# Macaron block on one core: attention's norm in one piece with four first projections, its last products turned about, and another order at the edges of the feed-forward layers

## The chip, the cores and the metric

One core of a Trainium2 chip. The metric is the device time of one execution in microseconds, median of three runs. One core has five engines with queues of their own: TensorE (PE, with its weight loads, PEld), VectorE (DVE), ScalarE (ACT), GpSimd (POOL) and SyncE (SP, here only DMA issues).

## The reference

A "macaron" block on x of 2 batches × 512 tokens × 512:

```python
x = x + 0.5 * ffn(layernorm(x))
x = x + attention(layernorm(x))      # 32 heads of 128, 8 KV heads, causal, no positions
x = x + 0.5 * ffn(layernorm(x))      # the same weights again
...
def ffn(x2):                          # 1024 tokens
    g_s, u_s = split(x2 @ shared_w_gate_up.T)              # 512 wide each
    shared_out = silu(g_s) * u_s @ shared_w_down.T
    w = top2(softmax(x2 @ gate_w.T)); w = w / sum(w)        # 16 experts
    moe_out = sum_e w_e * (silu(g_e) * u_e @ w_down_e.T)    # 128 wide each
    return moe_out + shared_out
```

Everything is float32.

## The kernel before

Each float32 product is made of three fp32r products of split operands, `PARTS = ((0,0),(0,1),(1,0))`: a "high" part, which ScalarE makes by a copy (`..._hi`), and a "low" part, the difference, which DVE or POOL subtracts (`..._lo`). So each product has, in front of it, a copy and a subtraction on two other engines. PSUM has eight banks, each named in the code.

x lies in SBUF as 8 tiles of 128 tokens (tiles 0 to 3 are batch 0, 4 to 7 batch 1). Each of the five engines runs a program written out by hand in one block (`block.tensor`, `.vector`, `.scalar`, `.gpsimd`, `.sync`); the order in each is the order of issue, and semaphores with counted values tie them together. Nothing is scheduled by a planner.

**A feed-forward layer** (n = 0 before attention, n = 1 behind it). The norm goes in two halves (`normalise`, L832 to 854; `turn_norm` on TensorE, L1188; `turned_norm` on ScalarE L571 and DVE L864). The shared part has 8 slots s: slice s//2 of the inner width and batch s%2. For each: `gate_up` (gate half, then up half, 12 matmuls each, L1252), silu (`gate`, ACT L608), `multiply` (DVE L969), `high` (ACT L614), `low` (DVE L974), `down` (12 matmuls, 3 for each tile, L1271), `add_down` (DVE, four adds, L962). A slice's weights are cut by `cut_gu` and `cut_dn` (ACT L592, L599) and `low_gu`, `low_dn` (DVE L941, L948; POOL L465, L471), from `raw_w[0]` or `raw_w[1]`, into one pair of buffers `wgu`, `wdn` (slice 3's down weights into `wdn_late`). Slots 0 to 4 come before the routed tiles, 5 to 7 behind them.

The router's logits are matmuls (`router`, L1199), copied by ScalarE (L578), folded and turned by 16 small matmuls (L1210), which lie between the router and `gate_up(1)`; DVE finds the top two (L881 to L895), `rank` (L1284, L1288, issued in the second half of `gate_up(1)`) counts, DVE makes row numbers (L905 to L916). POOL scatters the normalised tokens to `x_rows` in DRAM by 16 indirect DMAs (L509), TensorE goes on with shared slots 2 to 4, and then come 31 tiles of 128 sorted rows (`routed`): SP loads a tile into `xn` (L331), TensorE turns it (L1299), ScalarE copies (`turned`, L634) and DVE subtracts (L997), the expert's weights are cut as a front part (ACT L638, DVE L1003) and a back part (ACT L644, POOL `back` L481), gate and up (L1338), silu, product, `turn_hidden` (L1314), y (L1349), `y_out` (DVE L1021), store (SP L336). After the last tile POOL gathers the rows back by 16 indirect DMAs (L520), two for each tile of tokens, and DVE adds them with their weights (`combine`, L1044, two tiles of tokens to a call, m = 0 and 1 each). In the first layer POOL stops after the 12th gather until 8 combine adds are done, makes four of the six low parts of attention's first weights (`first_cuts`, L545; the key's, the value's and four queries' weights), then issues the last four gathers and the two low parts left.

The order on TensorE behind the tiles:

```python
gate_up(n, BEFORE + 1)                 # slot 5
pe.wait_ge(moe[n].y_out, TILES)
down(n, BEFORE)                        # slot 4
gate_up(n, SLOTS - 2)                  # slot 6
gate_up(n, SLOTS - 1, (0,))            # slot 7, gate
down(n, SLOTS - 2)
gate_up(n, SLOTS - 1, (1,))            # slot 7, up
down(n, BEFORE + 1)
if n == 0:
    turn_norm(1, 0)
down(n, SLOTS - 1)
```

**Attention** has 64 units u (8 KV heads × 2 batches × 4 query heads) in a software pipeline of slots (`att_slots`: the first and last written out, a loop between). In slot u TensorE does: scores S(u) (L1394, L1398), turns of unit u-1's probabilities (L1376), the projection of a later query (L1363), the last turns of u-1, the dense product of an earlier unit (L1432, 12 matmuls into one token tile of x), PV of u-1 (L1444, L1448), and in some slots the projection of a key or value. Masks and maxima are DVE's (L1071), exponentials ScalarE's (L732), the division POOL's (L538), the high and low parts of probabilities ACT L706 and DVE L1051, of queries and outputs ACT L711, L744 and DVE L1055, the dense adds DVE L1091. Ahead of slot 0: key, value, `project(wqs[0])` into bank 4 (after `add_down(7)`), the value's turn. After slot 1's PV: the norm's second half, `turn_norm(1, 1)`, in two pairs of tiles, which wait for each other's low parts, and behind it key 1.

SP issues the weights of layer 1 once the last in-loop product is done (o_mm ≥ 64), on both sides of the change.

## Time and profile before

| | us |
|---|---|
| median of 3 runs (1162.78 to 1164.62) | 1164.51 |
| the profiled execution, its own time | 1161.62 |
| its span, first to last instruction | 1159.9 |
| TensorE busy | 1110.0 |
| DVE busy | 670.8 |
| ScalarE busy | 571.6 |
| POOL busy | 465.4 |

The mean granted clock of TensorE is 0.988 of full. A row of a timeline has start, duration, engine, line, operation, what is written from what is read, and in brackets the idle time of the engine before it and what ended it. "issue" there is time in which the engine waited for nothing that the profile shows, "remote" a release that comes from none of the recorded instructions. A start is counted from the span's first instruction. Matmul ends are modelled.

### The profile page before, as it was taken

What the parts mean: (1) busy time and instruction counts of PE and PEld (TensorE: products, weight loads), DVE (VectorE), ACT (ScalarE), POOL (GpSimd) and SP (SyncE); (2) the same over time, 40 slices, a digit from 0 to 9 for tenths busy, and PEclk for the clock granted to TensorE, in tenths of its full rate; (3) what the DMA queues carried; (4) which work ended last, traced back from release to release, by engine and by line L of the source; (5) the groups of instructions that cost most, each with busy time, mean ns of one, the idle gap of its engine ahead of it and who ended that gap; (6) DMA issues with size and microseconds to landing.
All of it is one profiled execution on the core that took longest, in us unless ns stands there. A gap on an engine that the chain in (4) does not pass through costs nothing.

```text
span 1159.9 us, 19606 instructions
## 1 busy us (share of the span) xinstructions
PE 1110.0 (96%) x6008; PEld 930.1 (80%) x6008; DVE 670.8 (58%) x1810; ACT 571.6 (49%) x1514; POOL 465.4 (40%) x484
## 2 busy tenths in 40 slices
PE   8889998799999999999999999999999998899996
PEld 6667876588888888888888888888888876678875
DVE  7568867744545444545454445454454547668866
ACT  4257752555546445545444454544553533257750
POOL 1546647125315315324423432522532320546644
PEclk9989999999999999999999999999999999999998
DMA  9985565001101101000110010010000006935556
GB/s 357 414 325 190 186 225 185 16 1 37 56 1 37 55 0 36 22 32 0 36 54 0 36 54 0 36 54 0 36 0 1 1 1 269 372 112 176 189 157 197
DMA packets 38617, 114.80 MB, mean 99 GB/s; under 512 B 4384, under 2 KB 4384, under 8 KB 36512
## 3 DMA queue, kind: packets, MB, share of 16 engines
q1 hardware_dynamic: 33440, 97.30, 23.1%
q0 software_dynamic: 5120, 16.78, 4.2%
q8 instruction: 30, 0.49, 0.2%
q14 instruction: 27, 0.22, 0.1%
HBM read 79.20 MB, written 34.87 MB: 98 GB/s over the span
## 4 chain that ended last, share of the span: by engine, by line
PE 89%; DVE 4%; issue 3%; ACT 2%; DMA 1%; DVEq 0%; SPq 0%; ACTq 0%
PE bank L1363 23%; PE bank L1432 15%; PE bank L1448 9%; PE bank L1398 9%; PE bank L1338 7%; PE bank L1252 6%; PE bank L1376 6%; PE bank L1349 4%; PE bank L1271 3%; PE bank L1299 2%; PE bank L1444 1%; PE bank L1394 1%; DMA xn<-x_rows 1%; PE bank L1231 1%; PE bank L1188 1%
## 5 line engine op out<-in xcount | busy, mean ns | idle before, releaser
L538 POOL TENSOR_TENSOR scores<-scores,pinv 128x512 f32<-128x512 f32 (+3 forms) x256 | 176.7, 723 | 360.6 <-DVE pinv L1081 360.6
L481 POOL TENSOR_TENSOR tback_lo<-experts,tback_hi 128x768 fp32r<-128x768 f32 x62 | 114.3, 1845 | 82.4 <-ACT tback_hi L644 82.4
L744 ACT ACTIVATE oT_hi<-bank 128x512 fp32r<-128x512 f32 x64 | 38.3, 598 | 208.7 <-PE bank L1444 208.7
L732 ACT ACTIVATE scores<-scores,nmax 128x512 f32<-128x512 f32 (+3 forms) x256 | 140.3, 558 | 0.6 <-DVE nmax L1071 0.5
L706 ACT ACTIVATE pT_hi<-bank 128x512 fp32r<-128x512 f32 (+2 forms) x192 | 86.8, 487 | 108.0 <-PE bank L1376 108.0
L1051 DVE TENSOR_TENSOR pT_lo<-bank,pT_hi 128x512 fp32r<-128x512 f32 (+2 forms) x192 | 100.9, 553 | 48.3 <-ACT pT_hi L706 48.3
L1071 DVE CUSTOM_DVE_ANT_0 scores<-bank,causal 128x512 f32<-128x512 f32 (+3 forms) x256 | 112.2, 486 | 1.5 <-issue 0.5
L1363 PE MATMUL bank<-xnT_hi,wqs_hi 128*128 128x512 f32 x256 | 106.4, 416 | 0.9 <-DVE x L962 0.9
L1432 PE MATMUL bank<-wds_hi,oT_hi 128*128 128x512 f32 x256 | 105.9, 414 | 1.4 <-DVE oT_lo L1055 1.4
L1055 DVE TENSOR_TENSOR oT_lo<-bank,oT_hi 128x512 fp32r<-128x512 f32 x64 | 44.3, 691 | 108.6 <-ACT oT_hi L744 108.6
L1363 PE MATMUL bank<-xnT_lo,wqs_hi 128*128 128x512 f32 x256 | 100.8, 394 | 0.0
L1363 PE MATMUL bank<-xnT_hi,wqs_lo 128*128 128x512 f32 x256 | 100.8, 394 | 0.0
L1432 PE MATMUL bank<-wds_hi,oT_lo 128*128 128x512 f32 x256 | 100.6, 393 | 0.0
L1432 PE MATMUL bank<-wds_lo,oT_hi 128*128 128x512 f32 x256 | 99.5, 389 | 0.0
L1376 PE MATMUL bank<-ident,scores 128*128 128x128 f32 x640 | 90.8, 272 | 2.4 <-DVE pT_lo L1051 2.4
L1376 PEld LDWEIGHTS bank<-ident,scores 128*128 128x128 f32 x640 | 75.4, 141 | 11.0 <-DVE pT_lo L1051 2.8
L1091 DVE TENSOR_TENSOR x<-bank,x 128x512 f32<-128x512 f32 x64 | 44.1, 691 | 64.8 <-PE bank L1432 64.8
L1398 PE MATMUL bank<-kT_hi,qT_hi 128*128 128x512 f32 (+2 forms) x192 | 73.1, 381 | 2.2 <-DVE qT_lo L1055 2.2
L545 POOL TENSOR_TENSOR wqs_lo<-raw_q,wqs_hi 128x512 fp32r<-128x512 f32 x32 | 41.3, 1295 | 76.1 <-ACT wqs_hi L680 75.1
L1448 PE MATMUL bank<-pT_hi,vv_hi 128*128 128x512 f32 (+2 forms) x192 | 65.5, 341 | 1.6 <-DVE pT_lo L1051 1.6
L1398 PE MATMUL bank<-kT_hi,qT_lo 128*128 128x512 f32 (+2 forms) x192 | 65.1, 339 | 0.0
L1448 PE MATMUL bank<-pT_hi,vv_lo 128*128 128x512 f32 (+2 forms) x192 | 65.0, 339 | 0.0
(206 smaller groups left out, 2885.2 us busy)
## 6 DMA issues: line engine op xcount, KB each, us to landing
experts<-in_ffn_w SPq DMA_DIRECT2D x32, 768.0 KB
xn<-x_rows SPq DMA_DIRECT2D x62, 256.0 KB, 2.7
y_rows<-xn SPq DMA_DIRECT2D x62, 256.0 KB, 2.1
raw_q<-in_wq SPq DMA_DIRECT2D x8, 1024.0 KB
raw_d<-in_wd SPq DMA_DIRECT2D x8, 1024.0 KB
x_rows<-experts SPq DMA_DIRECT2D x1, 7936.0 KB, 29.7
raw_w<-in_ffn_w SPq DMA_DIRECT2D x8, 768.0 KB, 5.6
raw_kv<-in_wkv SPq DMA_DIRECT2D x8, 512.0 KB, 3.3
```

Of the source, the lines that this page charges most:

```text
L481: nc.gpsimd.tensor_tensor(tback[par][1][:], experts[:, bass.ds(at + FRONT, GU - FRONT)], tback[par][0][:].bitcast(F32), ALU.subtract).then ...
L538: nc.gpsimd.tensor_tensor(s, s, pinv[k % 2][:, i:i + 1].to_broadcast([P, P * (i + 1)]), ALU.mult).then_inc(att.normed, 1)
L706: nc.scalar.activation(pT[0][:, lo_col:hi_col], bank[b][:, 0:hi_col - lo_col], ACT.Copy).then_inc(att.t_hi, 1)
L732: nc.scalar.activation(s, s, ACT.Exp, bias=nmax[par][:, i:i + 1], scale=-1.0, accum_out=psumr[par][:, i:i + 1]).then_inc(att.exp, 1)
L1051: nc.vector.tensor_tensor(pT[1][:, lo_col:hi_col], bank[b][:, 0:hi_col - lo_col], pT[0][:, lo_col:hi_col].bitcast(F32), ALU.subtract).then ...
L1071: nc.vector.tensor_tensor_reduce(sp_[par][:, TRI[i]:TRI[i + 1]], bank[bk][:, c:c + w], causal[:, 512 - w:512], -SCORE_SCALE, 3.0e38, ALU.a ...
L1338: last = nc.tensor.matmul(bank[par][:, 0:2 * INTER], xT[par][a][:, c, :], piece[b][:, start:start + FRONT], start=(i == 0), stop=(i == 3 * ...
L1363: last = nc.tensor.matmul(into[:], w[a][:, c, :], xnT[z][:, c, b * SEQ:(b + 1) * SEQ], start=(m == 0), stop=(m == 3 * HC - 1))
L1376: last = nc.tensor.transpose(bank[b][:, at + (i - j) * P:at + (i - j + 1) * P], sp_[par][:, TRI[i] + j * P:TRI[i] + (j + 1) * P], ident[:])
L1398: last = nc.tensor.matmul(bank[bk][:, c:c + P * (i + 1)], qT[a][:, i * P:(i + 1) * P], kT[b][z][:, 0:P * (i + 1)], start=(m == 0), stop=(m ...
L1432: last = nc.tensor.matmul(o_bank(u)[:], oT[ob][h][a][:, tile * P:(tile + 1) * P], wds[h][z][:], start=(m == 0), stop=(m == 3 * G - 1))
L1448: last = nc.tensor.matmul(bank[1][:, j * P:SEQ], vv[bu][a][:, j, :], pT[z][:, COL[j]:COL[j] + SEQ - j * P], start=(j == 0 and m == 0), sto ...
```

## The change

It alters the order of work, buffers and semaphore counts, and the engine that makes six low parts; matmuls are as many as before.

- Router: the logits' banks are 1 and 4 (before 1 and 3); the 16 fold matmuls are issued after the first three matmuls of `gate_up(1)`, and `rank` one chunk later.
- Start of the tiles: the back part of tile 2 is cut ahead of the steps by ScalarE and POOL, `cut_dn(2)` moves to step 1, `add_down(3)` is split, two tiles of it in step 0. SP issues the loads of tiles 6 and 7 sooner, between experts' loads, and the raw weights of slice 3 before the tile loop; slice 3's gate and up weights have buffers of their own (`wgu_late`), cut at the last tile.
- End of the tiles and behind: the orders below. The six low parts of attention's first weights are DVE's (`first_lows`), and POOL's 16 gathers have no pause in them.
- Attention's start: key, value, queries 0 and 1 are projected into banks 0, 3, 1 and 2, the value is turned, `turn_norm(1, 1)` goes in one piece in banks 4 to 7, then come the slots; key 1 is projected in slot 0, query 2 in slot 1.
- Attention's end: from unit 63 on the dense product stands before the last turns, the wait for the last output's low part (`pv_lo`) comes only before its head, and the tail is cut by the norm of the next layer: slots 65 and 66, `turn_norm(2, 0)`, slots 67 and 68. The first gate and up of layer 1 wait for 61 and 63 adds (before 61 and 64).
- End of layer 1: `add_down(7)` in two pairs of tiles, about the combines; the stores of output tiles 2 and 3 wait for the combine adds.

```diff
-                    if j <= TILES - 2:
+                    if 0 < j <= TILES - 2:
...
@@ SP
-                for e in left[3:]:
+                for e in left[3:5]:
                     load_expert(e)
-                for k in range(4):
+                load_tile(n, 1, 2)
+                for e in left[5:]:
+                    load_expert(e)
+                store_tile(n, 0, 0)
+                load_tile(n, 1, 3)
+                for k in range(1, 4):
                     store_tile(n, 0, k)
-                    if k < 2:
-                        load_tile(n, 1, k + 2)
+                load_shared(n, 3)
                 with sp.Fori(2, TILES // 4) as it:
@@ POOL
                 back(0, at[1], 1)
+                back(1, at[2], 2)
                 low_dn(n, BEFORE // 2)
...
-                    if n == 0 and t == HALF + 1:
-
-                        pool.wait_ge(moe[n].added, 2 * HALF)
-                        first_cuts(low_part, 0, G)
...
-            pool.wait_ge(ffn[0].act_lo, SLOTS)
-            first_cuts(low_part, G)
+            pool.wait_ge(ffn[0].dn_lo, NSH)
@@ ACT, routed
                 front(at[1])
+                act.wait_ge(ffn[n].act_lo, BEFORE)
+                act.wait_ge(ffn[n].d_mm, HALF * (BEFORE - 1))
+                back(1, at[2], there[2] if n == 0 else 2 * LOADED_HALF)
                 turned(0, 1)
-
-                cut_dn(n, BEFORE // 2)
                 tile_steps(step)
@@ ACT, feed_forward
                 high(n, BEFORE)
-                shared(n, BEFORE + 1, SLOTS - 2)
+                gate(n, BEFORE + 1)
+                gate(n, SLOTS - 2)
+                cut_dn(n, NSH - 1)
                 if n == 0:
                     act.wait_ge(loaded.kv, 16)
                     first_cuts(high_part, 0, 2)
-                shared(n, SLOTS - 2, SLOTS - 1)
-                if n == 0:
                     act.wait_ge(loaded.q, 16)
                     first_cuts(high_part, 2)
+                high(n, SLOTS - 2)
+                high(n, BEFORE + 1)
                 gate(n, SLOTS - 1)
+                high(n, SLOTS - 1)
                 if n == 0:
                     roots(1, 0)
-                high(n, SLOTS - 1)
@@ DVE, feed_forward
                 multiply(n, BEFORE)
                 routed(n)
                 low(n, BEFORE)
+                if n == 0:
+                    first_lows(0, 2)
+                multiply(n, SLOTS - 2)
+                low_dn(n, NSH - 1)
+                if n == 0:
+                    first_lows(2, 4)
+                low(n, SLOTS - 2)
+                if n == 0:
+                    first_lows(4, 2 + G)
                 multiply(n, BEFORE + 1)
-                low_gu(n, NSH - 1)
                 low(n, BEFORE + 1)
-                low_dn(n, NSH - 1)
                 combine(n, 0)
-                multiply(n, SLOTS - 2)
-                low(n, SLOTS - 2)
+                add_down(n, SLOTS - 2)
+                multiply(n, SLOTS - 1)
                 combine(n, 2)
-                add_down(n, SLOTS - 2)
 
             feed_forward(0)
-            then = statistics(1, 0)
-            multiply(0, SLOTS - 1)
-            scaled(1, 0, then)
             low(0, SLOTS - 1)
+            normalise(1, 0)
             turned_norm(1, 0)
...
@@ PE, gate_up
+                if s == 1:
+
+                    pe.wait_ge(route[n].out, 1)
...
-                        if half == 1 and s == 1 and c == 1:
+                        if half == 0 and s == 1 and c == 1:
+                            fold_logits(n)
+                        if half == 1 and s == 1 and c == 2:
                             rank(n)
@@ PE, last tile step
                     if isinstance(j, int) and j == TILES:
+                        gate_up(n, BEFORE + 1, (0,), range(0, HC // 2))
                         turn_hidden(j, par)
+                        gate_up(n, BEFORE + 1, (0,), range(HC // 2, HC))
@@ PE, attention slot (dense is the old block as a function)
-                        if r == 1:
-                            pe.wait_ge(att.pv_lo, u - 1)
...
+                            if r == 1 and h == G - 1:
+                                pe.wait_ge(att.pv_lo, u - 1)
...
+                    if isinstance(u, int) and u == 0:
+                        pe.wait_ge(norm[1].lo, TT)
+                        project(wks, 1, PROJ_AHEAD)
+                    elif exists(u, 0, UNITS - 2):
...
+                    if isinstance(u, int) and u >= UNITS - 1:
+                        dense(g, u, k)
                     if exists(u, 1, UNITS):
                         pe.wait_ge(att.t_lo, 3 * (u - 1) + 1)
                         turn(1 - par, 2, 6, 0)
                         turn(1 - par, 3, 6, 256).then_inc(att.t_mm, 1)
...
-                    if isinstance(u, int) and u == 1:
-
-                        pe.wait_ge(att.proj_out, before + QPOS[1] + 1)
-                        turn_norm(1, 1)
-                        pe.wait_ge(norm[1].lo, TT)
@@ PE, attention
-                pe.wait_ge(ffn[0].added, HALF * (BEFORE + 2))
-                project(wqs[0], 0, 0, bank[4])
-                turn_value(2)
+                project(wqs[0], 0, 0, bank[1])
+                pe.wait_ge(att.w_lo, 4)
+                project(wqs[1], 0, 0, bank[2])
+                pe.wait_ge(att.v_first, 1)
+                turn_value(1)
+                turn_norm(1, 1)
                 att_slots(pe, slot)
-                att_tail(slot)
+                att_tail(slot, 1, 2)
+                turn_norm(2, 0)
+                att_tail(slot, 3, 4)
@@ PE, feed_forward
-                gate_up(n, BEFORE + 1)
+                gate_up(n, SLOTS - 2)
 
                 pe.wait_ge(moe[n].y_out, TILES)
                 down(n, BEFORE)
-                gate_up(n, SLOTS - 2)
-                gate_up(n, SLOTS - 1, (0,))
+                gate_up(n, BEFORE + 1, (1,))
                 down(n, SLOTS - 2)
-                gate_up(n, SLOTS - 1, (1,))
+                gate_up(n, SLOTS - 1)
                 down(n, BEFORE + 1)
+                down(n, SLOTS - 1, range(0, HALF // 2))
                 if n == 0:
                     turn_norm(1, 0)
-                down(n, SLOTS - 1)
+                down(n, SLOTS - 1, range(HALF // 2, HALF))
```

DVE's part of attention's start, of its end (`normalise(2, 0)`, slots 65 and 66, `turned_norm(2, 0)`, slots 67 and 68) and of the last layer (`low(7)`, `combine(4)`, half of `add_down(7)`, `combine(6)`, the other half) follows TensorE's order.

## Rows read from the trace of the kernel before

**Rows 1.** The page, busy time of each engine and the chain by engine
```profile
PE 1110.0 (96%) x6008; PEld 930.1 (80%) x6008; DVE 670.8 (58%) x1810; ACT 571.6 (49%) x1514; POOL 465.4 (40%) x484
...
PE 89%; DVE 4%; issue 3%; ACT 2%; DMA 1%; DVEq 0%; SPq 0%; ACTq 0%
```

**Rows 2.** Windows: stretch, us; each engine's busy us (count); granted clock; DMA share; GB/s
```profile
200.20:257.20 57.00, 49.57 (x258) 40.84 (x257) 35.93 (x109) 27.98 (x76) 12.04 (x17) 0.97 0.07 28
...
257.20:930.00 672.80, 672.80 (x3608) 580.27 (x3607) 334.08 (x1080) 334.93 (x997) 252.98 (x306) 1.00 0.07 25
```

**Rows 3.** Timeline of POOL, first scatter: start, us, instruction, idle before it
```profile
54.63 0.97 POOL L509 DMA_INDIRECT x_rows<-xn,rows  x1 [0.30 <-issue]
```

**Rows 4.** Timeline of ScalarE, first scatter
```profile
58.22 0.60 ACT L608 ACTIVATE sg<-bank 128x512 f32<-128x512 f32 x1 [7.23 <-remote]
```

**Rows 5.** Chain of waits in order of time, its long pieces: start, us, what
```profile
37.09 5.59 PE bank L1252 x24
...
172.64 8.39 PE bank L1252 x36
...
231.85 4.38 PE bank L1363 x12
```

**Rows 6.** Timeline of ScalarE, first gather
```profile
186.50 0.60 ACT L608 ACTIVATE sg<-bank 128x512 f32<-128x512 f32 x1 [2.66 <-remote]
```

**Rows 7.** Timeline of POOL, first gather
```profile
171.84 1.29 POOL L520 DMA_INDIRECT yg<-y_rows,rows  x1 [0.31 <-issue]
...
183.60 1.03 POOL L520 DMA_INDIRECT yg<-y_rows,rows  x1 [0.30 <-issue]
```

**Rows 8.** Timeline of ScalarE, second gather
```profile
1137.76 0.60 ACT L608 ACTIVATE sg<-bank 128x512 f32<-128x512 f32 x1 [0.87 <-issue]
```

**Rows 9.** Timeline of DVE, second gather
```profile
1147.41 0.69 DVE L969 TENSOR_TENSOR sg<-sg,bank 128x512 f32<-128x512 f32 x1 [3.77 <-remote]
```

**Rows 10.** Timeline of POOL, second gather, its first and last transfer
```profile
1125.70 0.99 POOL L520 DMA_INDIRECT yg<-y_rows,rows  x1 [9.69 <-DMA y_rows<-xn]
...
1146.13 0.95 POOL L520 DMA_INDIRECT yg<-y_rows,rows  x1 [0.30 <-issue]
```

**Rows 11.** Timeline of TensorE, first routed tiles
```profile
75.78 0.36 PE L1338 MATMUL bank<-tfront_hi,xT_hi 128*128 128x256 f32 x1 [1.94 <-DVE tfront_lo L1003]
...
87.89 0.66 PE L1299 MATMUL bank<-ident,xn 128*128 128x128 f32 x4 [0.95 <-DMA xn<-x_rows]
```

**Rows 12.** Timeline of TensorE, norm ahead of attention
```profile
194.19 3.43 PE L1188 MATMUL bank<-ident,xn 128*128 128x128 f32 x16 [3.03 <-DVE xn L854]
```

**Rows 13.** Timeline of DVE, ahead of that norm
```profile
186.55 2.48 DVE L962 SCALAR_TENSOR_TENSOR x<-bank,x 128x512 f32<-128x512 f32 x4 [1.42 <-PE bank L1271]
...
189.07 2.47 DVE L832 BATCH_NORM_STATS2 stats<-x 128x6 f32<-128x512 f32 x4
```

**Rows 14.** Timeline of TensorE, attention's start
```profile
211.22 0.50 PE L1398 MATMUL bank<-kT_hi,qT_hi 128*128 128x512 f32 x1 [0.90 <-DVE qT_lo L1055]
...
217.44 0.50 PE L1398 MATMUL bank<-kT_hi,qT_hi 128*128 128x512 f32 x1 [1.34 <-DVE qT_lo L1055]
...
226.26 0.39 PE L1448 MATMUL bank<-pT_hi,vv_hi 128*128 128x256 f32 x1 [1.65 <-DVE pT_lo L1051]
...
229.22 1.22 PE L1188 MATMUL bank<-ident,xn 128*128 128x128 f32 x8 [1.23 <-DVE xnT_lo L864]
...
231.85 0.79 PE L1363 MATMUL bank<-xnT_hi,wks_hi 128*128 128x512 f32 x1 [1.41 <-DVE xnT_lo L864]
```

**Rows 15.** Timeline of TensorE, attention's end
```profile
951.93 0.55 PE L1376 MATMUL bank<-ident,scores 128*128 128x128 f32 x3 [1.25 <-DVE pT_lo L1051]
...
958.46 0.50 PE L1432 MATMUL bank<-wds_hi,oT_hi 128*128 128x512 f32 x1 [1.41 <-DVE oT_lo L1055]
...
972.78 0.48 PE L1231 MATMUL bank<-xnT_hi,wgu_hi 128*128 128x512 f32 x1 [1.40 <-issue]
```

**Rows 16.** Timeline of POOL, attention's end
```profile
946.85 2.76 POOL L538 TENSOR_TENSOR scores<-scores,pinv 128x512 f32<-128x512 f32 x4 [7.49 <-DVE pinv L1081]
```

More of the change, by code:

```diff
@@ L146, in build @@
                 yg = sb("yg", [P, TT, 2, HID], F32, sub)
-            oT = [[pair(f"oT0_{r}", [P, SEQ], st) for r in range(G)], [None] * G]
+            oT = [[None] * G, [pair(f"oT1_{r}", [P, SEQ], st) for r in range(G)]]
             pT = pair("pT", [P, TRI[ST]], st)
@@ L160, in build @@
             kT[1] = pair("kT1", [P, SEQ], st)
-            oT[1][0] = pair("oT1_0", [P, SEQ], st)
-            oT[1][1:] = [pair(f"oT1_{r}", [P, SEQ], st) for r in range(1, G)]
+            oT[0][G - 1] = pair(f"oT0_{G - 1}", [P, SEQ], st)
+            oT[0][:G - 1] = [pair(f"oT0_{r}", [P, SEQ], st) for r in range(G - 1)]
             vT = sb("vT", [P, SEQ], F32, st)
@@ L261, in att_slots, with att_tail @@
                 slot(KV - 1, k)
-        def att_tail(slot):
-            for k in range(8 + 1, 8 + 5):
+        def att_tail(slot, first, last):
+            for k in range(8 + first, 8 + last + 1):
                 slot(KV - 1, k)
         def o_bank(u):
-            return bank[(0, 1, 3, 2)[u - UNITS - 1] if isinstance(u, int) and u > UNITS else 2]
+            return bank[(0, 1, 2, 3)[u - UNITS - 1] if isinstance(u, int) and u > UNITS else 2]
         UNITS = KV * BATCH * G
@@ L603, in gate @@
                 act.wait_ge(f.g_mm, s + 1)
-                wait(act, f.act_lo, s - 1)
+                if s >= 2:
+                    act.wait_ge(f.act_lo, DOWN_AT[s - 2] + 1)
                 if s == 1:
@@ L1015, in step @@
                                                 ALU.mult).then_inc(m.mul, 1)
+                    if j == 0:
+                        add_down(n, BEFORE - 1, range(HALF // 2, HALF))
+                    if j == TILES:
+                        low_gu(n, NSH - 1)
                     if exists(j, 1, TILES):
@@ L1028, in routed @@
                 turned(0, 1)
-                add_down(n, BEFORE - 1)
+                add_down(n, BEFORE - 1, range(HALF // 2))
                 dve.wait_ge(route[n].scattered, 2 * TT * 16)
@@ L1184, in turn_norm @@
                     pe.wait_ge(norm[n].mul, t + 1)
-                    wait(pe, norm[n].lo, t - 1 if n == 1 and h == 1 else t - 3)
+                    if n != 1:
+                        wait(pe, norm[n].lo, t - 3)
                     for c in range(HC):
@@ L1378, in turn, with dense @@
                     return last
+                def dense(g, u, k):
+                    if exists(u, 5, UNITS + 4):
+                        r = k % 4
+                        ob = (0, 1, 1, 1, 1, 0, 0, 0)[k % 8]
+                        tile = (r - 1) % 4
+                        wait(pe, att.added, UNITS - HALF if isinstance(u, int) and u > UNITS else u - 5)
+                        m = 0
+                        for h in range(G):
+                            if k == 5:
+                                pe.wait_ge(att.w_lo, 6 + 10 * g + (3 if exists(u, 0, UNITS - 9) else 1) + h)
+                            if r == 1 and h == G - 1:
+                                pe.wait_ge(att.pv_lo, u - 1)
+                            for a, z in PARTS:
+                                last = nc.tensor.matmul(o_bank(u)[:], oT[ob][h][a][:, tile * P:(tile + 1) * P],
+                                                        wds[h][z][:], start=(m == 0), stop=(m == 3 * G - 1))
+                                m += 1
+                        last.then_inc(att.o_mm, 1)
                 def slot(g, k):
@@ L1391, in slot @@
                             wait(pe, att.masked, 4 * (u - 1) + (1, 3, 4)[n])
+                            if isinstance(u, int) and u == 0:
+                                wait(pe, norm[1].lo, (0, HALF + 1, HALF + 2)[n])
                             for i, c in tiles:
```

214 lines of the change are left out of this document (122 added, 92 removed).

## The prediction

> **What bounds the kernel now.** I read the page first. TensorE is busy for 1110.0 of 1159.9 us, and the chain that ended last is 89% TensorE [rows 1]; no other engine is above 58%. The change alters no matmul, so it can act only through TensorE's idle time, 50 us in all, and through its clock. The table of windows says where that is: none in attention's loop, where TensorE is busy for 672.80 of 672.80 us, and 7.4 us at attention's start [rows 2]; the rest is at attention's very end and in the two feed-forward layers. The timelines then give each wait a place and a releaser.
>
> One thing needs care before any sum. POOL issues the 16 indirect transfers of the first scatter, each 0.97 us with 0.30 between, the last at 54.63 [rows 3]. In the later part of such a run TensorE's signals seem to reach the others late. ScalarE's silu of shared slot 3 waits 7.23 us and starts at 58.22, just after the run, released by something that the trace calls remote [rows 4]. In the first gather, which began at about 169.3, a stretch of 36 matmuls ends at 181.03 (172.64 and 8.39) [rows 5]; the silu behind it starts only at 186.50, after a remote wait [rows 6], when POOL's pause had begun at 184.63 (183.60 and 1.03) [rows 7]. In the second gather, which has no pause, the silu at the same place starts at once, 12.1 us into the run (1137.76 against 1125.70), but DVE's last multiplication waits 3.77 us on something remote and starts at 1147.41, as the run ends (1146.13 and 0.95) [rows 8 to 10]. I read: late in a run TensorE's signals are held until the run ends or pauses; it began before 11.7 us in the first gather, after 12.1 in the second.
>
> **The change part by part.** One 512-column matmul costs 0.233 us (5.59 for 24 [rows 5]).
>
> *Router.* The 16 fold matmuls come three matmuls later, 0.7 us, and what covers the copy they wait for was idle time anyway. So row numbers, scatter and all that hangs on the scatter's end [rows 3, 4] come about 0.65 later in each layer: a loss of 1.3. Bounds: 0 (the restart does not follow) and -1.4.
>
> *Start of the routed tiles.* The weights of tile 2 are cut before the steps, and the adds of shared slot 3 are split in two. The 1.94 us wait for DVE's front part [rows 11] goes, but tile 2 waits for the same chain (copy of back(1), turned, POOL's back), and I leave it about half: +1.05 per layer. The tile load moved before the last experts takes away the 0.95 us wait for data at 87.89 [rows 11] in the first layer. Together +3.05. Bounds: 0, if tile 2 inherits all, and 2 × 1.94 + 0.95 = 4.8.
>
> *End of the first layer.* Before: gate-up 5, down 4, gate-up 6, gate 7, down 6, up 7, down 5, norm, down 7. After: gate 5 around the last tile's turn, gate-up 6, down 4, up 5, down 6, gate-up 7, down 5, half of down 7, norm, the other half. What ends last in both is DVE's work up to the first normalised row, for which TensorE stands 3.03 us and starts at 194.19 [rows 12]. The six subtractions of attention's first weights move from POOL to DVE (0.69 each, as its operations of this size [rows 9]), 4.1 us more, ahead of the adds. DVE's list from low 4 on is now fourteen operations of 0.69 (9.7), two combines of four such (2.75 each), four adds (2.48), four statistics (2.47) [rows 13] and 2.5 more to the first row (194.1 less the statistics' end at 191.54): 22.6 us. With its waits for gathers and ScalarE I get the first row at 194.8 against 194.1; but half of down 7 is then done before the norm, 1.4 us that stood behind it. If signals come in time, attention so starts some 0.4 earlier: +0.4. But the gather now has no pause. It starts 1.9 later, since gate 5 (2.8) stands before the last tile's product and not behind it, at 171.2, and its 16 transfers end at about 192 (15 × 1.27 + 0.95, one or two of them lengthened). The last multiplication stands on a signal of TensorE that leaves about 14.5 us into the run, and behind it in DVE's queue stand combine 2, low 7 and the norm: 0.7 + 2.75 + 0.7 + 5.0 = 9.1 us to the first row, so at 201, 6 later than in time. That gives 0.4 - 6 = -5.6. The lower bound, with add_down 6 held as well, is 3 us worse, -8.6; the upper is +0.4. I take -5.6, since the first gather already held a signal at 11.7 us [rows 5, 6].
>
> POOL's gathers and DVE meet here in another way: the transfer at 171.84 took 1.29 us [rows 7], while DVE subtracted two SBUF tensors; the last of the second gather took 0.95 [rows 10]. The Trainium skill (Trainium Architecture — The Big Picture, What this means for kernel authors) says that the port pair shared by DVE and GpSimd is an exclusive lock and not a split of bandwidth, and so speaks against the move of the six subtractions. The trace agrees for this one transfer. By that rule the six would lengthen the run by 6 × 0.34, some 2 us, and the sum would be as much smaller, which lies inside the bounds above.
>
> *Attention's start.* Four first projections (key, value, two queries) fill the stretch in which DVE ends the second half of x; then comes the norm of the other four tiles in one piece, and key 1 sits in slot 0. Gone are the waits of 0.90, 1.34, 1.65, 1.23 and 1.41 us, and the slow passage of key 1's 12 matmuls after them, 4.38 against 2.8 at the full clock: 1.6 [rows 5, 14]. That is 8.1. New: DVE's queue behind the first norm is eight combines (5.5), four adds, statistics and scaling (2.5, 2.5, 2.5), which ends some 1.9 us behind the four projections (48 matmuls, 11.2) and the value's turn; and S(1) waits for the low parts of the second query and of key 1, about 1.8. 8.1 - 3.7 = +4.4. Bounds: +1 (the norm's wait brings the half clock to what follows it, and each new wait is about a microsecond longer) and +6.2 (no wait at S(1)).
>
> *Attention's end.* Products before turns cover the 1.25 wait; the wait for the last head's low part, 1.41, comes behind 9 of 12 matmuls; the norm in the middle of the tail fills the 1.40 before the first gate [rows 15]: 4.06 at most. The slot before gains nothing: POOL's four divisions end at 949.61 (946.85 and 2.76) [rows 16], and the turn behind them can't be earlier. I take +3.3, bounds +1.4 and +4.1. The experts of the second layer are asked for at the same product as before and hide under its router.
>
> *End of the second layer.* The last multiplication's signal leaves earlier in the run (about 14.5 us instead of 17.8). In time, the end comes 1.8 earlier; held to the end of a run that starts 1.9 later and with adds split about the combines, 3.7 later. I take -0.4, between, since this gather held nothing at 12.
>
> **Sum.** -1.3 + 3.05 - 5.6 + 4.4 + 3.3 - 0.4 = +3.45 us. The profiled execution took 1161.6 us beside its span of 1159.9; the change's would take 1158.2. The runs' median is 1164.5, 2.9 above; less 3.45 that is 1161.1.
>
> The Trainium skill (TensorE: Matmul & The Clock Gate, Part 1: The HAM clock gate) puts it that the default state is throttled and activity releases the throttle. The 4.38 after idle fits [rows 5, 14]. By that rule any wait left at attention's start costs more than itself, which would put that part nearer its lower bound.
>
> **The rivals.**
> - *Signals come in time* in the unpaused gathers. For it: the second gather held nothing at 12.1 us. Against: the first did at 11.7. The sum is -1.3 + 3.05 + 0.4 + 4.4 + 3.3 + 1.8 = 11.65: 1152.9 us.
> - *Slower: the run without a pause holds DVE's queue to its end* in both layers, one mechanism at its two places: -8.6 and -3.7 instead of -5.6 and -0.4. The sum is -2.85: 1167.4 us. It decides once the two together cost over 9.5, the sum of the other parts. For it: the 7.23 us in the scatter, which is such a run [rows 4]. Against: the second gather [rows 8].
> - *Attention's start doesn't do what it says*: each removed wait comes back as the wait for the norm and at S(1), at half clock, +1 instead of +4.4. Total 0.05: 1164.5 us.
>
> **How the numbers follow.** Chances: my forecast 0.42, signals in time 0.28, slower by the hold 0.18, start unchanged 0.12. About 0.2% (2.3 us) is what a measurement of this kernel can tell from no change: 1162.2 to 1166.8. The forecast's own range, 1157 to 1165, has about a third above 1162.2, so faster is 0.29 + 0.28 = 0.57; same is 0.13 of the forecast, 0.08 of the unchanged start and 0.02 of the slower case, 0.23; slower is the rest, 0.20. The range goes from 1152, past the case in time, to 1167.5, past the slower one.
>
> **What the changed profile would show.** In the first gather 16 transfers without a pause from about 171, DVE's last multiplication at 191 to 195 with a remote wait, and the first projection at 205 to 207; if that is at 200, the rival in time holds. From the first projection to the third unit's scores 4.4 us less. The last slots and the first gate of the second layer 3.3 closer. The 1.94 wait gone, a smaller one at tile 2. The prediction is wrong if the signals are not tied to POOL's run at all, or if a split product or the moved loads of shared weights bring a wait into the tiles, where I put none.

## The result: 0.5% slower, and where the profile puts it

The changed kernel takes 1171.1 us (median of 20 runs) against 1165.4 us (20 runs): ratio 1.0047, interval [1.0032, 1.0063]. One run of each kernel was far slower than the rest (1836.98 and 1246.07 us) and is left out of the ratio. The forecast was 1161.1 and a range up to 1167.5; the sign was wrong and the time lies outside the range.

The page of the changed kernel, the same two rows as [rows 1]:

```profile
PE 1112.9 (95%) x6008; PEld 932.1 (80%) x6008; DVE 674.5 (58%) x1815; ACT 569.6 (49%) x1513; POOL 458.0 (39%) x478
...
PE 81%; DVE 5%; another core or an unknown queue 4%; issue 3%; ACT 3%; DMA 2%; POOL 0%; SPq 0%; DVEq 0%; ACTq 0%
```

TensorE works nearly as long as before, but the chain has a new part, 4% "another core or an unknown queue": time in which an engine waited and none of the recorded instructions released it. The windows of the changed kernel, cut at the first tile's turn, the last tile's turn, the first projection, the second layer's first gate, and again the two turns (columns as in [rows 2]):

```profile
0.00:71.70 71.70, 58.25 (x279) 45.91 (x280) 43.49 (x123) 24.41 (x38) 21.25 (x34) 0.93 0.93 359
71.70:160.95 89.25, 86.02 (x560) 69.06 (x558) 71.54 (x120) 63.31 (x146) 55.14 (x31) 0.98 0.64 222
160.95:211.64 50.69, 40.25 (x175) 31.44 (x173) 31.52 (x60) 15.40 (x29) 18.49 (x19) 0.87 0.51 187
211.64:974.78 763.14, 758.31 (x4066) 651.95 (x4064) 393.79 (x1254) 377.33 (x1112) 272.89 (x331) 1.00 0.07 24
974.78:1032.09 57.31, 48.67 (x220) 37.01 (x219) 34.87 (x101) 17.75 (x27) 18.51 (x18) 0.94 0.82 325
1032.09:1117.85 85.76, 84.50 (x559) 68.16 (x558) 72.54 (x120) 63.16 (x146) 54.52 (x30) 1.00 0.53 176
1117.85:1168.30 50.45, 36.89 (x158) 28.56 (x156) 26.78 (x43) 8.29 (x17) 17.20 (x17) 0.88 0.46 146
```

Beside them the lengths of the same stages before:

| stage | before | after | difference | forecast |
|---|---|---|---|---|
| layer 1, to the first tile | 69.5 | 71.7 | +2.2 | +0.65 |
| its tiles | 87.2 | 89.3 | +2.0 | -2.0 |
| its end, to the first projection | 43.4 | 50.7 | +7.3 | +5.6 |
| attention, to the next layer's first gate | 772.6 | 763.1 | -9.4 | -7.7 |
| layer 2, to the first tile | 55.0 | 57.3 | +2.3 | +0.65 |
| its tiles | 85.6 | 85.8 | +0.1 | -1.05 |
| its end | 46.5 | 50.5 | +4.0 | +0.4 |
| span | 1159.9 | 1168.3 | +8.4 | -3.45 |

Attention gives more than forecast; the two feed-forward layers lose it, and more. (The profiled execution before, 1161.6 us, lay 3.8 us below the median of its 20 runs, so the two traces differ by more than the medians do. Stages of single traces vary too: the first stage, with the same code as before, took 71.1 and 71.6 us in the traces of att_only and before_nopause below. A difference of 2 us in one stage is not told from that.) The longest waits stand at POOL's four runs of 16 transfers. ScalarE's timeline:

```profile
54.86 0.60 ACT L627 ACTIVATE sg<-bank 128x512 f32<-128x512 f32 x1 [7.69 <-remote]
59.93 1.06 ACT L610 ACTIVATE wgu_hi<-raw_w 128x1024 fp32r<-128x1024 f32 x1 [4.47 <-remote]
...
196.99 0.60 ACT L627 ACTIVATE sg<-bank 128x512 f32<-128x512 f32 x1 [13.42 <-remote]
...
1153.47 0.60 ACT L627 ACTIVATE sg<-bank 128x512 f32<-128x512 f32 x1 [13.64 <-remote]
```

TensorE's timeline, what it stands for behind them (the second row is a wait among the tiles, for tile 8's rows):

```profile
62.30 0.79 PE L1315 MATMUL bank<-xnT_hi,wgu_hi 128*128 128x512 f32 x1 [8.00 <-DVE wgu_lo L977]
...
96.77 0.66 PE L1362 MATMUL bank<-ident,xn 128*128 128x128 f32 x4 [2.62 <-DMA xn<-x_rows]
...
201.71 0.77 PE L1334 MATMUL bank<-wdn_late_hi,ab_hi 128*128 128x512 f32 x1 [7.22 <-DVE ab_lo L1013]
206.31 3.67 PE L1244 MATMUL bank<-ident,xn 128*128 128x128 f32 x16 [1.70 <-DVE xn L889]
...
1023.70 0.80 PE L1315 MATMUL bank<-xnT_hi,wgu_hi 128*128 128x512 f32 x1 [7.86 <-DVE wgu_lo L977]
...
1158.18 0.77 PE L1334 MATMUL bank<-wdn_late_hi,ab_hi 128*128 128x512 f32 x1 [8.70 <-DVE ab_lo L1013]
```

And on POOL the last transfer of the first scatter and of the first gather:

```profile
56.62 0.97 POOL L528 DMA_INDIRECT x_rows<-xn,rows  x1 [0.30 <-issue]
...
193.68 0.94 POOL L539 DMA_INDIRECT yg<-y_rows,rows  x1 [0.30 <-issue]
```

The order in the first gather is: the transfers end at 194.62, and 2.4 us later, at 196.99, the silu of slot 7 begins, whose matmuls were over at about 187. Behind the silu come on DVE the multiplication (197.62), which also needs the up half, over at about 190, then combine 2, low 7 and the norm, until TensorE turns it at 206.31; in [rows 12] that was 194.19. In the second gather the transfers end at 1150.88 and the silu begins at 1153.47, 2.6 us later. Before, it began at 1137.76 there [rows 8].

Not every late signal waits for the run's end. In the first scatter the silu of slot 3 starts at 54.86, 6.1 us after its matmuls (over at 48.74) but 2.7 us before the run ends (57.59); only the next signal, that of the up half, is held past the end, and with it the cut of weights at 59.93, for which TensorE stands until 62.30. The trace of before had such releases inside a run too: its DVE and ScalarE both end a remote wait at 50.35, with the run ending at 55.60. So "held until the run ends or pauses", as the prediction read it, is too simple: signals become late, by 5 us and more, some pass while the run goes on, and the last ones come behind it.

### The profile page after: what moved, and what is told of

It reads as the page before. It is cut to its first block, busy times and chain, and to the rows that moved or that the text cites. A ratio compares the mean times of both kernels' runs of the same rounds, so it can differ in the third digit from the quotient of the medians.

```text
span 1168.3 us, 19604 instructions
## 1 busy us (share of the span) xinstructions
PE 1112.9 (95%) x6008; PEld 932.1 (80%) x6008; DVE 674.5 (58%) x1815; ACT 569.6 (49%) x1513; POOL 458.0 (39%) x478
## 4 chain that ended last, share of the span: by engine, by line
PE 81%; DVE 5%; another core or an unknown queue 4%; issue 3%; ACT 3%; DMA 2%; POOL 0%; SPq 0%; DVEq 0%; ACTq 0%
PE bank L1428 22%; PE bank L1460 14%; PE bank L1529 9%; PE bank L1489 8%; PE bank L1403 7%; PE bank L1441 6%; PE bank L1414 4%; PE bank L1315 3%; PE bank L1362 2%; PE bank L1525 1%; PE bank L1485 1%; DVE x L1087 1%; PE bank L1288 1%; DMA xn<-x_rows 1%
## 5 line engine op out<-in xcount | busy, mean ns | idle before, releaser
L560 POOL TENSOR_TENSOR wqs_lo<-raw_q,wqs_hi 128x512 fp32r<-128x512 f32 x28 | 36.3, 1295 | 75.2 <-ACT wqs_hi L703 75.2
L1414 PE MATMUL bank<-experts,hT 128*128 x124 | 64.5, 601 | 0.6 <-ACT hT L675 0.3
```

What stands on the lines that cost most here:

```text
L1414: last = nc.tensor.matmul(bank[6 + 1 - par][:], hT[:], experts[:, bass.ds(at[k] + GU, HID)], start=True, stop=True)
```

## The experiments

All ratios are to the kernel before, timed beside each on the same chip, where its median was 1165.2 to 1168.2 us. The changed kernel was not timed again there. A difference from it, or between two of the kernels below, is therefore taken between their two ratios (0.001 is 1.2 us) and carries the error of both, some 3 to 5 us.

**1 and 2. The change in two halves.** One kernel has only attention's edges (the norm in one piece with four first projections, the products turned about, the norm in the tail), the other all the rest. In short:

```diff
 att_only: before, with these
+                project(wqs[0], 0, 0, bank[1]); project(wqs[1], 0, 0, bank[2])
+                turn_value(1); turn_norm(1, 1)
...
+                att_tail(slot, 1, 2); turn_norm(2, 0); att_tail(slot, 3, 4)
 ffn_only: before, with every other hunk of the diff
```

> The kernel before with attention's two edges alone changed (four first projections, the norm in one piece, the products turned about, the norm within the tail); the feed-forward layers keep their order. Theory (the loss is all in the feed-forward layers, since POOL's runs of transfers hold TensorE's signals): attention's edges gave 9.4 us between the first projection and the next layer's first gate (763.1 against 772.6), so 9 us faster than before, ratio 0.992. Rival (attention's new start only looks quick because it begins after a longer stand, with more of DVE's work already behind it): 3 to 5 us faster.

> The rest of the change alone: router, start of the tiles, order behind them, the first weights' low parts on DVE, no pause in the gather; attention as before. Theory: the two layers lost 11.4 and 6.4 us, so 15 to 18 us slower than before, ratio 1.014. Rival (the loss comes from the two halves together): under 8 us slower.

att_only: 1156.9 us, ratio 0.9934 [0.9912, 0.9955], 7.7 us faster. ffn_only: 1181.5 us, ratio 1.0142 [1.0107, 1.0177], 16.5 us slower. The gain at attention's edges is real and stands alone (its trace has 761.8 us for that stage, as the changed kernel has 763.1); the loss is all in the feed-forward layers' part. In sum, 8.8, the halves lose 3 us more than the whole, which is within the error of the three ratios.

**3. A pause in the gathers.**

```diff
                         ).then_inc(gathered[t], 16)
+                    if t == HALF + 1:
+                        pool.wait_ge(moe[n].added, 2 * HALF)
```

> The changed kernel with POOL stopping after the 12th of its 16 gathers, in both layers, until eight combine adds are done, as the first layer did before; nothing else. Theory (a run holds the signals until it pauses): the silu of slot 7 starts about 2 us after the 12th transfer, near 191.5 instead of 197 in the first layer, and as much earlier in the second; 5 to 8 us faster than the changed kernel. Rival (the signals are late for another reason, such as TensorE's instruction fetch or traffic): the silu stays at 197 and the kernel gets 0 to 4 us slower by the late gathers.

1165.9 us, ratio 0.9996 [0.9976, 1.0017], 6 us faster than the changed kernel. Its timelines, POOL and then ScalarE:

```profile
191.40 0.95 POOL L539 DMA_INDIRECT yg<-y_rows,rows  x1 [0.30 <-issue]
198.56 1.15 POOL L539 DMA_INDIRECT yg<-y_rows,rows  x1 [6.21 <-DVE x L1089]
```

```profile
194.32 0.60 ACT L629 ACTIVATE sg<-bank 128x512 f32<-128x512 f32 x1 [7.42 <-remote]
```

The 12th transfer ends at 192.35, the silu starts 2.0 us later, with four transfers still to come; in the second layer it is 1145.90 and 1147.96. So it is the run on POOL that holds the signal, and a pause lets it through.

**4. A pause in the scatters**, until the first eight have landed.

```diff
                             in_=xn[:, t, :], in_offset=None).then_inc(route[n].scattered, 16)
+                    if t == HALF - 1:
+                        pool.wait_ge(route[n].scattered, 2 * HALF * 16)
```

> The changed kernel with POOL stopping after the 8th of the 16 scatters, in both layers, until those eight have landed; nothing else. Theory (a run holds the signals): the silu of slot 3 and what follows are released within about 2 us of the matmuls' end, TensorE's stand of 8 us before slot 4 shrinks to 1 or 2, though the scatter ends 2 to 3 us later and the first tile may wait for it; 4 to 10 us faster in all. Rival: the stands stay at 8 us and the scatter's end is later, 4 to 6 us slower.

1171.6 us, ratio 1.0051 [1.0030, 1.0072]: no gain. But the mechanism shows. ScalarE has no remote wait in the scatter any more, and slot 4 no stand. What takes its place is the first tile's data:

```profile
56.79 0.97 POOL L528 DMA_INDIRECT x_rows<-xn,rows  x1 [9.69 <-DMA x_rows<-xn,rows]
```

```profile
71.22 1.09 PE L1364 MATMUL bank<-ident,xn 128*128 128x128 f32 x4 [10.05 <-DMA xn<-x_rows]
```

Eight transfers took 9.7 us more to land, the scatter ended at 66.7 and no longer at 57.6, and TensorE waits 10.05 us for the tile (in the second layer the eight took 8.0). The theory held, the remedy was too long; my expectation of 2 to 3 us for the landing was wrong.

**5 and 6. Short pauses**, made by waiting for the very signals that would be held. On the changed kernel in all four runs, on att_only in the scatters and the second gather (there after the 10th and the 14th).

```diff
                             in_=xn[:, t, :], in_offset=None).then_inc(route[n].scattered, 16)
+                    if t == HALF:
+                        pool.wait_ge(ffn[n].g_mm, 4)
+                    if t == HALF + 1:
+                        pool.wait_ge(ffn[n].u_mm, 4)
...
                         ).then_inc(gathered[t], 16)
+                    if t == HALF:
+                        pool.wait_ge(ffn[n].g_mm, 8)
+                    if t == HALF + 1:
+                        pool.wait_ge(ffn[n].u_mm, 8)
```

> The changed kernel; in each of the two scatters POOL waits after the 10th transfer for TensorE's signal of slot 3's gate and after the 12th for that of its up half, and in each of the two gathers at the same places for slot 7's. These signals are due at that moment anyway, so that the waits are short if a pause lets them through. Theory: the stands of 8.0 and 7.9 us before slot 4 fall to about 2 to 3, those of 7.2 and 8.7 before down 7 to about 2 to 4; 12 to 18 us faster than the changed kernel, near 1155. Rival (only a pause until the transfers have landed helps, or the pauses cost as much as they save): within 4 us of it.

> The kernel with attention's two edges alone changed, and the same waits of POOL in the two scatters and, in the second layer, after the 10th gather and the 14th. Theory: the stands of 7.1 and 5.0 us before slot 4 and of 3.8 before down 7 shrink to a third; 8 to 12 us faster than without the waits (1156.9), near 1147. Rival: within 2 us of it.

after_selfwait: 1148.1 us, ratio 0.9849 [0.9812, 0.9886]: 23 us faster than the changed kernel, more than expected. att_selfwait: 1146.2 us, ratio 0.9836 [0.9797, 0.9875], 11 us faster than att_only. The pause is 2 us long, and ends with the signal. POOL and ScalarE in after_selfwait, first scatter:

```profile
53.16 0.96 POOL L528 DMA_INDIRECT x_rows<-xn,rows  x1 [1.94 <-remote]
```

```profile
52.92 0.60 ACT L635 ACTIVATE sg<-bank 128x512 f32<-128x512 f32 x1 [4.32 <-remote]
```

With the hold eased, the two orders of the feed-forward layers are 2 us apart (ratios 0.9849 and 0.9836), which is not told from nothing; without, 13 us (1.0047 and 0.9934). So some 12 us of the change's loss are the hold, which the new order runs into.

**7. The short pauses in the gathers alone.**

> The changed kernel with POOL's two short waits for TensorE's signals in the two gathers only; the scatters run through as in the change. Theory (both kinds of run hold signals, the gathers' hold is what the change made worse): 10 to 13 us faster than the changed kernel, near 1159, and the rest of the 23 us of the run with waits in all four belongs to the scatters, which the kernel before had too. Rival (the gain is the scatters'): 3 to 5 us faster.

1160.0 us, ratio 0.9935 [0.9910, 0.9959]: 13 us faster than the changed kernel. The other 10 us are the scatters', and the kernel before has such a hold in them too [rows 4].

**8. The pause taken from the kernel before.**

```diff
-                    if n == 0 and t == HALF + 1:
-                        pool.wait_ge(moe[n].added, 2 * HALF)
-                        first_cuts(low_part, 0, G)
...
+            first_cuts(low_part, 0, G)
             pool.wait_ge(ffn[0].act_lo, SLOTS)
```

> The kernel before with one edit: POOL's pause after the 12th gather of the first layer is gone, and the four low parts made in it follow the last gather. Theory (the run then holds slot 7's silu to about 191.5 instead of 186.5, but in this order DVE takes the multiplication only at 192, behind the statistics): within 2 us of before. Rival (the lost pause alone makes the loss of the first layer): 5 to 8 us slower.

1169.5 us, ratio 1.0019 [0.9999, 1.0040], 2 us slower, at the edge of what can be told. The held signal is not the expected one: the silu of slot 7 comes in time, at 186.32. The hold now stands elsewhere, at the adds of slot 6:

```profile
191.65 0.69 DVE L959 SCALAR_TENSOR_TENSOR x<-bank,x 128x512 f32<-128x512 f32 x1 [2.84 <-remote]
```

The old order has its multiplication of slot 7 behind the statistics, where a held signal has time; the changed one has it ahead of combine 2 and the norm. How the loss divides between the pause and the order stays open. By the medians the missing pause costs 2 us. By this trace the end of the first layer is 49.1 us long, 5.6 more than before (the changed kernel's is 50.7), and the attention stage behind it gives 2.4 of that back (770.2 against 772.6). Set back into the changed kernel (experiment 3), the pause brings that end to 45.8.

**9. POOL's run interrupted by POOL itself.** After every fourth transfer four small memsets, each waiting for the one before, 1.06 us in all, and no wait for another engine.

```diff
+                    if t % 2:
+                        for i in range(4):
+                            wait(pool, breathed, taken[0])
+                            nc.gpsimd.memset(breath[:], float(i)).then_inc(breathed, 1)
+                            taken[0] += 1
```

> The changed kernel; after every fourth transfer of each run POOL makes four small memsets, each waiting for the one before (some 1 us in all), and waits for no other engine. Theory A (any interruption of POOL's run lets TensorE's signals through): the silu of slot 7 starts by 191 instead of 197, the stands before slot 4 and down 7 fall to under 4 us, 8 us or more faster than the changed kernel. Theory B (the signals pass only in a pause of about 2 us, or when fewer transfers are under way): the stands stay and the longer runs make it 2 to 6 us slower.

1156.9 us, ratio 0.9899 [0.9873, 0.9925], 17 us faster than the changed kernel, though each run is 3 us longer. Its trace has no remote wait at all. The silu of slot 7:

```profile
186.57 0.60 ACT L640 ACTIVATE sg<-bank 128x512 f32<-128x512 f32 x1 [3.50 <-PE bank L1328]
```

So nothing in TensorE's work or its queue made the signals late, and no other engine need be waited for: in this run 1.2 us without a transfer's issue every 5 us were enough. What in the issue of transfers holds the signals, this doesn't show.

**10. Where slice 3's weights are loaded.** Behind the tile loop (after_sh3); and, with the short pauses, behind the row load of the last tile (combo1).

```diff
-                load_shared(n, 3)
                 with sp.Fori(2, TILES // 4) as it:
...
                     if k < TILES % 4:
                         load_tile(n, last, k)
+                    if k == TILES % 4 - 1:
+                        load_shared(n, 3)
```

> The changed kernel with the load of slice 3's weights behind the tile loop on SyncE's queue, and no longer ahead of the load of tile 8. Theory (those 768 KB stand ahead of tile 8's rows): the wait of 2.6 us for tile 8 falls to about 1; 1.5 us faster than the changed kernel. Rival (the moved loads of tiles 6 and 7 are what made tile 8 late): the wait stays.

> The changed kernel with the short waits in all four runs, and slice 3's weights loaded behind the row load of the last tile. Theory (those 768 KB delay the rows of tiles 8 and 9, and of tile 28 where they stood behind the loop): tile 8's wait goes and none comes at 28, 2 us faster than with the waits alone (1148.1), near 1146. Rival (the weights then come too late for the cut at the last tile, or tile 8 is late by the loads of tiles 6 and 7): same or slower.

after_sh3: 1171.9 us, ratio 1.0050 [1.0025, 1.0076], no gain: the wait of 2.62 us for tile 8 is gone, but tile 28's rows now come late (4.35 us from turn to turn in layer 2 where 2.84 is the rule). combo1: 1146.1 us, ratio 0.9815 [0.9785, 0.9845], 4 us below after_selfwait by the ratios and 2 by the medians, within the error; in its trace there is no wait at tile 8 and none at 28 (one of 0.67 us at tile 27).

**11. The fold's place.** Fold and ranks one chunk earlier, as before the change, on the changed kernel and on combo1.

```diff
-                        if half == 0 and s == 1 and c == 1:
+                        if half == 0 and s == 1 and c == 0:
                             fold_logits(n)
-                        if half == 1 and s == 1 and c == 2:
+                        if half == 1 and s == 1 and c == 1:
                             rank(n)
```

> The changed kernel with the 16 fold matmuls and the ranks one chunk earlier, where they were before. Theory (the later fold costs 0.7 to 1.1 us per layer and the restart behind the scatter follows it): 1.5 to 2.5 us faster than the changed kernel. Rival (the restart is set by the hold and not by the fold): within 1 us.

> The best kernel so far (the change with short waits in all four runs and the weights of slice 3 loaded last, 1146.1) with the 16 fold matmuls and the ranks back in their old place. Theory: with the hold gone, TensorE stands for the first tile's rows, so for the scatter's end, and the fold's 0.65 us per layer comes out in full: 1.3 us faster. Rival: the place of the fold is without effect, within 0.5 us.

after_fold: 1171.1 us, ratio 1.0034 [1.0006, 1.0062], not to be told from the changed kernel, against the expectation. combo1_fold: 1143.7 us, ratio 0.9795 [0.9773, 0.9817], 2.3 us below combo1, though the intervals overlap; that the fold's place pays once the hold is gone is so not shown. It has the lowest time of this study, 2.0% under the kernel before and 2.5% under the changed one.

The trace of after_fold shows which signal decides. In its first gather, which ends at 195.37, ScalarE and DVE have

```profile
191.37 0.60 ACT L627 ACTIVATE sg<-bank 128x512 f32<-128x512 f32 x1 [7.04 <-remote]
...
197.90 0.69 DVE L1008 TENSOR_TENSOR sg<-sg,bank 128x512 f32<-128x512 f32 x1 [7.80 <-remote]
```

The gate half's signal passes inside the run, and the multiplication waits all the same, for the up half's, until 2.5 us behind the run: as late as in the changed kernel (197.62).

## Why the prediction was wrong

*The step that failed*, as far as experiments show it, is the size taken for the hold at the ends of the two feed-forward layers: -5.6 and -0.4 us, where -7.3 and -4.0 were measured. Two more terms missed in the traces, the router and the start of the tiles. Between the two traces, in us of gain:

| term | forecast | measured |
|---|---|---|
| router | -1.3 | -4.5 |
| start of the tiles | +3.05 | -2.2 |
| the two layers' ends (the hold) | -6.0 | -11.2 |
| attention | +7.7 | +9.4 |

The hold's full size stood in the prediction as the rival "the run without a pause holds DVE's queue", with -8.6 and -3.7 for the two ends, 12.3 in all; the measured 11.2 is nearer to that than to the forecast's 6.0. So the mechanism and its full price were right. What failed was the value taken for the second layer, "between, since this gather held nothing at 12", and the chance of 0.18 for the full size. The prediction's values in time were right as well: with short pauses in the gathers alone (after_gself), the two ends are 42.9 and 44.4 us, 0.5 and 2.1 less than before, for forecasts of 0.4 and 1.8. That the tiles lose is seen in traces only, and the terms of the router and the tiles together miss by more than the hold does (8.4 against 5.2); as single stages vary by some 2 us between traces, a part of that may be chance. The rival of the full hold put the time at 1167.4 with the other parts as forecast, still 3.7 short.

- *Router.* Forecast 1.3 us of loss, measured +2.2 and +2.3 in the stages up to the first tile. The scatters start 1.1 and 1.0 us later into their stages, where the fold's place was priced at 0.65; but in att_only, where this part is untouched, the first starts at 36.80, later than in the changed kernel. The runs themselves are 0.9 us longer (21.1 against 20.3 and 20.2), which the prediction had not seen. Their first transfer now starts inside a subtraction of DVE; before, it started ahead of it. DVE's and POOL's rows, changed kernel and then before:

```profile
36.06 1.22 DVE L977 TENSOR_TENSOR wgu_lo<-raw_w,wgu_hi 128x1024 fp32r<-128x1024 f32 x1
...
36.45 1.86 POOL L528 DMA_INDIRECT x_rows<-xn,rows  x1 [32.37 <-DVE rows L951]
```

```profile
35.31 1.16 POOL L509 DMA_INDIRECT x_rows<-xn,rows  x1 [31.23 <-DVE rows L916]
...
35.53 1.22 DVE L941 TENSOR_TENSOR wgu_lo<-raw_w,wgu_hi 128x1024 fp32r<-128x1024 f32 x1 [0.52 <-ACT wgu_hi L592]
```

The transfer ends 1.03 us after the subtraction (37.28 to 38.31). In the second layer it takes 1.76 against 1.05, and with the fold back in its old place (combo1_fold against combo1) 1.16 and 1.05 against 1.86 and 1.76. TensorE stands 8.0 us at each scatter of the changed kernel. Before, it stood 6.5 in the first one, 3.85 before slot 4 and the rest in pieces marked "issue", and 4.7 in the second; in att_only 7.1 and 6.5. So the two short stands of before's trace are in part its own. The step "the restart hangs on the run of transfers" was right.
- *Start of the tiles.* Forecast 3.05 of gain, measured 2.2 of loss. The first half was near in the first layer: the turn from tile 2 to 3 fell from 5.02 to 3.70 us and the next rose from 2.84 to 3.30, a gain of 0.86 for a forecast of 1.05; in the second layer the turn to tile 2 took 0.42 more, which leaves 0.42. The prediction kept no price for the 768 KB of slice 3, which SyncE now asks for ahead of tile 8's rows: the turns of tiles 8 and 9 come 5.68 and 4.26 us behind the ones before them, and 2.84 is the rule. It had named the moved load as what could break it, and put nothing on it. That this load makes tile 8 late is shown by after_sh3, where the wait is gone.
- *End of the first layer.* Forecast -5.6, measured -7.3, between the forecast and its lower bound. The last multiplication was to come at 191 to 195 and came at 197.62; the first projection was to come at 205 to 207 and came at 211.64. The gather started 5.0 us later, not 1.9, 4.2 of it inherited from the earlier stages. The held signal came 2.4 us behind the run's end; the prediction had it at the end. With short pauses in all four runs this stage takes 43.2 us, 0.2 less than before, near the in-time value of +0.4.
- *Attention's start and end.* Forecast 7.7, measured 9.4 in the stage and 7.7 by att_only's ratio. The new waits are 1.02 for the norm, 0.40 at key 1 and 1.54 at S(1), 3.0 in place of 3.7; the slow passage at key 1 is gone (its 12 matmuls take 3.1 us, from 228.68 to 231.75, against 4.38). At the end, the last two rows, 0.92 and 0.61 us are left of the three waits of 4.06.

```profile
224.45 2.03 PE L1244 MATMUL bank<-ident,xn 128*128 128x128 f32 x16 [1.02 <-DVE xn L889]
...
228.68 0.50 PE L1428 MATMUL bank<-xnT_hi,wks_hi 128*128 128x512 f32 x1 [0.40 <-DVE xnT_lo L899]
...
233.29 0.50 PE L1489 MATMUL bank<-kT_hi,qT_hi 128*128 128x512 f32 x1 [1.54 <-DVE qT_lo L1105]
...
955.30 0.98 PE L1441 MATMUL bank<-ident,scores 128*128 128x128 f32 x7 [0.92 <-POOL scores L553]
...
967.43 2.03 PE L1244 MATMUL bank<-ident,xn 128*128 128x128 f32 x16 [0.61 <-DVE xn L889]
```

- *End of the second layer.* Forecast -0.4, measured -4.0, the price of the full hold (-3.7). "This gather held nothing at 12 us" was true of the gate half of slot 7 alone. The multiplication waits for the up half as well, whose signal left 17.8 us into the run before and was held (3.77 us of remote wait [rows 9]); in the new order it leaves 15.8 us into the run, after the gate half's at 12.97, whose silu starts only behind the run's end; the multiplication came at 1154.10. That a gate half's signal can pass without helping the multiplication is what after_fold shows in the first layer. So the ground for a value in between spoke of a signal that did not decide.
- *The Trainium skill's rule* (Trainium Architecture — The Big Picture, What this means for kernel authors) that the port pair shared by DVE and GpSimd is an exclusive lock would have made the gather 2 us longer by the six subtractions. The 16 gathers took 20.4 us from first start to last end (174.25 to 194.62), and 19.9 in the second layer (1130.95 to 1150.88), which has no such subtractions: 0.5 us. Where an instruction of each meets, the rule fits: a transfer that starts inside a 1.22 us subtraction takes 1.86 or 1.76 us. In the gathers few meet.

What stays open: why a run of these transfers holds TensorE's signals, why it sets in some 9 to 13 us into one (in the first gather of the changed kernel a signal that left 9.3 us into the run, at 183.57, let an add begin only at 188.47), and why some signals pass inside the run. The runs show only that a pause or the end lets them through. Whether the new order costs anything beside the hold, the fold included, is not told from the noise.

## What to carry to other kernels

A wait that something "remote" ends just after another engine's long run of issues is a bound of its own: before moving work, look at what signals must cross such a run, and break the run by a short pause before they are due. A pause is cheap (1 to 2 us here) where it covers only the signal, and dear (8 to 10 us) where it waits for data to land. Ask of a held wait which of its signals comes last: evidence on another signal of the same slot says little. And one trace of a wait whose length changes from run to run is no basis for a value between two bounds; where the mechanism shows at nearly every place of its kind, the full price deserves more than a small chance.

## What the runs showed of the hardware that was not expected

- Signals of TensorE that fall due late in a run of POOL's indirect transfers (128 rows of 2 KB each, 0.95 to 0.97 us and 0.30 between) reach ScalarE, DVE and POOL 5 us and more late. Most come 1.5 to 2.7 us after the run ends or pauses: 192.35 to 194.32, 194.62 to 196.99, 1150.88 to 1153.47. Some pass while the run goes on: 54.86 in a run that ends at 57.59, 191.37 in one that ends at 195.37. Breaks of 1.2 us after every fourth transfer (1.06 of memsets) leave no such wait.
- Short pauses give back 23 of 1171 us in the changed kernel and 11 of 1157 in att_only, whose feed-forward layers are those of the kernel before.
- An indirect transfer that starts inside a DVE subtraction of two SBUF tensors (1.22 us) takes 1.86 and 1.76 us; one that starts ahead of it 1.16 and 1.05.
- Eight such scatters beside the experts' loads take 9.7 us to land after the last is issued, 8.0 in the second layer.
